# A graph kernel on one core: the row of numbers for the degree one-hots moves from SBUF into a PSUM bank

## The reference

```python
xn = _layernorm(x)
# layer 0, graph part: theta(x_dst - x_src) + phi(x_src), relu, max over the edges of a node
e = relu((xn[dst] - xn[src]) @ theta.T + theta_b + xn[src] @ phi.T + phi_b)
x = x + where(isfinite(segment_max(e, dst)), ..., 0) + mix0(xn)   # mix0: attention over features, MLP
x = x + experts(layernorm(x))                                     # 8 experts, gated
# layer 1, graph part: three rounds of a mean over neighbours; the mean needs the degree of each node
deg = segment_sum(ones, dst)
mean = segment_sum(h[src], dst) / maximum(deg, 1)
x = x + sage(...) + mix1(...); x = x + ffn(layernorm(x))
```

## Time and profile before

| | us |
|---|---|
| median of three runs | 2274.82 |
| the profiled execution, device time | 2287.81 |
| span of its trace, first to last instruction | 2286.0 |
| PE / DVE / ACT / POOL busy in the span | 1742.0 / 1300.6 / 594.1 / 1173.6 |
| mean granted TensorE clock | 0.849 |
| POOL gathers L273, x400, busy | 523.9 |
| DVE scans L526, x399, busy | 192.9 |

### The profile page before, as it was taken

The page is one execution under the profiler, slowest core; times in us unless marked ns, Lnnn a source line. Parts: engine busy times, 40 slices in busy tenths (PEclk is TensorE's granted clock), DMA queues, the critical chain, the costliest instruction groups (busy, mean ns, idle before and its releaser), DMA issues. The chain is left out here.

```text
span 2286.0 us, 25612 instructions
## 1 busy us (share of the span) xinstructions
PE 1742.0 (76%) x8399; PEld 1010.7 (44%) x8399; DVE 1300.6 (57%) x2567; ACT 594.1 (26%) x937; POOL 1173.6 (51%) x888
## 2 busy tenths in 40 slices
PE   7985454635552746999999259699989999997996
PEld 6862122212221513555555138655565556544543
DVE  6878666766775644777777244545541221115995
ACT  4001001100111124666666131321120010003453
POOL 0888888878886777888888857300000000000343
PEclk9557777777785868999999667899999999997998
DMA  6257688887868202111110020154424443531002
GB/s 171 62 141 196 184 222 216 216 228 211 227 191 206 60 2 51 36 34 33 33 33 13 1 66 2 19 124 108 108 50 119 126 96 92 127 79 38 1 7 78
DMA packets 193170, 229.06 MB, mean 100 GB/s; under 512 B 66574, under 2 KB 174178, under 8 KB 187697
## 3 DMA queue, kind: packets, MB, share of 16 engines
q1 hardware_dynamic: 125887, 172.58, 28.2%
q0 software_dynamic: 67200, 55.46, 11.0%
HBM read 148.81 MB, written 78.24 MB: 99 GB/s over the span
## 5 line engine op out<-in xcount | busy, mean ns | idle before, releaser
L706 POOL DMA_INDIRECT adjacency<-all_cell_val,all_cell_idx x400 | 546.3, 1366 | 151.2 <-issue 120.4
L273 POOL DMA_INDIRECT edge_ring<-b_rows,all_src_idx x400 | 523.9, 1310 | 174.3 <-issue 172.5
L1659 POOL TENSOR_TENSOR ffn_hl<-ffn_hid,ffn_hh 128x448 f16<-128x448 f32 x56 | 70.0, 1252 | 737.9 <-ACT ffn_hid L1676 737.9
L1472 PE MATMUL bank<-sage_adj,sage_zh 125*128 125x448 f16 x1050 | 370.1, 352 | 3.4 <-DVE sage_zl L1526 3.4
L1472 PE MATMUL bank<-sage_adj,sage_zl 125*128 125x448 f16 x1050 | 370.0, 352 | 0.0
L526 DVE SCALAR_TENSOR_TENSOR edge_ring<-edge_ring,w_keep 125x256 f32<-125x256 f32 x399 | 192.9, 484 | 142.6 <-DMA edge_ring<-b_rows,all_src_idx 122.3
L1549 DVE TENSOR_TENSOR sage_u<-bank,w_rd 128x448 f32<-128x448 f32 x42 | 26.2, 624 | 236.2 <-PE bank L1477 233.4
L1472 PEld LDWEIGHTS bank<-sage_adj,sage_zh 125*128 125x128 f16 x1050 | 102.6, 98 | 101.8 <-issue 8.0
L1472 PEld LDWEIGHTS bank<-sage_adj,sage_zl 125*128 125x128 f16 x1050 | 102.7, 98 | 99.6 <-issue 5.8
L681 DVE SCALAR_TENSOR_TENSOR edge_junk<-bank,all_key_c,all_later 125x400 f16<-125x400 f32 x232 | 145.6, 627 | 0.0
L820 PE MATMUL bank<-all_a,w_W1h 128*128 (+1 forms) x448 | 122.5, 355 | 25.0 <-ACTq L1115 25.0
(11 more groups left out here) (423 smaller groups left out, 3598.8 us busy)
## 6 DMA issues: line engine op xcount, KB each, us to landing
sage_adj<-adjacency SPq DMA_DIRECT2D x105, 490.0 KB
run_max<-edge_ring SPq DMA_DIRECT2D x40, 1120.0 KB
adjacency<-edge_zero SPq DMA_DIRECT2D x25, 714.0 KB
experts_gb<-gate_rows SPq DMA_DIRECT2D x56, 224.0 KB
edge_ring<-b_rows,all_src_idx POOLq DMA_INDIRECT x400
adjacency<-all_cell_val,all_cell_idx POOLq DMA_INDIRECT x400
sage_adj<-adjacency SPq DMA_DIRECT2D x105, 56.9 KB
run_max<-edge_ring SPq DMA_DIRECT2D x40, 130.0 KB
```

The costliest lines, as they stand in the source:

```text
L273: nc.gpsimd.indirect_dma_start(ring[:, k % RING, :], None, dram.rows[:, :], bass.IndirectOffsetOnAxis(ap=c.src_idx[:, k:k + 1], axis=0)).t ...
L706: nc.gpsimd.indirect_dma_start(dram.adj_flat, bass.IndirectOffsetOnAxis(ap=c.cell_idx[:, k:k + 1], axis=0), c.cell_val[:, k:k + 1], None). ...
L1472: ins = mm(ps[4 * b + h][:, 0:T], z[:, g * JG + j, half(h)], adj[g][:, j, :], start=(g == 0 and j == 0 and z is zh), stop=False)
L1659: nc.gpsimd.tensor_tensor(hl[:, m, :], hid[:, m, :], hh[:, m, :], ALU.subtract).then_inc(low, 1)
```

## The change

A row of 125 numbers is copied to PSUM once, into the last columns of bank 6, and both comparisons read it there. So that bank 6 holds nothing else meanwhile, the `b` rows take banks 4, 5 and 7 in turn, and `b_rows(j)` waits for copy j-3 instead of j-4.

```diff
+        b_bank = lambda j: (4, 5, 7)[j % 3]
+        row_p = ps[6][0:B, 2 * D - P:2 * D - P + B]
...
                     pe.wait_ge(taken, 4 * (j // 4) + 4)
-                    if j >= 4:
-                        pe.wait_ge(b_out, j - 3)
+                    if j >= 3:
+                        pe.wait_ge(b_out, j - 2)
                     for k in range(KH):
-                        ins = mm(ps[4 + j % 4][0:B, 0:D], c.yn[:, k, B * j:B * (j + 1)], wb[:, k, :], start=(k == 0), stop=(k == KH - 1))
+                        ins = mm(ps[b_bank(j)][0:B, 0:D], c.yn[:, k, B * j:B * (j + 1)], wb[:, k, :], start=(k == 0), stop=(k == KH - 1))
...
-                            nc.scalar.copy(xt[:, j, :], ps[4 + j % 4][0:B, 0:D]).then_inc(b_out, 1)
+                            nc.scalar.copy(xt[:, j, :], ps[b_bank(j)][0:B, 0:D]).then_inc(b_out, 1)
...
                 dve.wait_ge(edges_in, 80)
+                v.tensor_copy(row_p, c.row[0:B, 0:B])
                 v.tensor_copy(src_f[:], c.src_idx[:])
...
                         v.tensor_tensor(oh_hi[:, e, :], hi[:, e].unsqueeze(2).to_broadcast([B, 5 * HOT, NB]),
-                                        c.row[0:B, 0:NB].unsqueeze(1).to_broadcast([B, 5 * HOT, NB]), ALU.is_equal)
+                                        row_p[:, 0:NB].unsqueeze(1).to_broadcast([B, 5 * HOT, NB]), ALU.is_equal)
...
                     v.tensor_tensor(oh_lo[:, g % 2], lo[:, g * HOT:(g + 1) * HOT].unsqueeze(2).to_broadcast([B, HOT, B]),
-                                    c.row_b[:].unsqueeze(1).to_broadcast([B, HOT, B]), ALU.is_equal).then_inc(hot_ready, 1)
+                                    row_p.unsqueeze(1).to_broadcast([B, HOT, B]), ALU.is_equal).then_inc(hot_ready, 1)
```

## The result

Five runs of the change took 2257.4 to 2259.92 us, median 2259.52; before, beside them, 2276.1 us. The medians lie 16.6 us apart; the ratio, which is not that of the medians, is 0.992, 95% interval 0.9903 to 0.9937. A later set on another chip gave 0.994 (0.9925 to 0.9955). The forecast was 2261.2 us, a gain of 13.6 us and a ratio of 0.994.

A forecast was written before the change was run, and what follows sets the result against it. GpSimd issuing 400 gathers was taken to bound the stage, losing 28.0 us early to stretches. A 14.4 us gain at gather 49 less 0.8 for later stretches made 13.6: 2274.8 to 2261.2 us, range 2252 to 2274.

The forecast's parts named there:

- The place of the row: Early gathers starting inside comparisons: reading the row from PSUM ends their stretching, worth 0 to 28.0 us.
- What was late next: Gathers 44 to 49 wait for TensorE to free `xn` tiles; gather 49 starts at 142.1, a gain of 14.4 us.
- TensorE's turns and the comparison's price: In the gather stage, TensorE's turns stay 3.84 us and a comparison reading a bank costs 0 extra.
- rival 4: Comparisons read a broadcast row from a bank at half rate, 4.3 instead of 2.15 us: slower, 2301 us; chance 4%.
- The copy and the banks: Row copy takes 0.3 us, hidden by a 2.22 us wait; three banks for b rows cause no wait, at most 2.2.
- Behind gather 49: Later gathers: ring slots suffice, VectorE catches up, and denser scans add 0.8 us of stretches, bounds 0 and 3.
- The stages behind the barrier: Stages after the gather stage hang on its end and on nothing absolute; no size given.
- Rival 1: The row's place is of no account, something else in the comparison blocks GpSimd: time 2274.8 us; chance 5%.
- Rival 2: Gain is real in the gather stage but partly given back behind it: 2265 to 2269 us; chance 15%.
- Rival 3: TensorE's turns run at full clock, gather 49 starts at about 131: a gain of 25, 2250 us; chance 5%.

The follow-up runs named there:

- three kernels with more room for tiles of `xn` or earlier `grams`: Against the change: ring of 56 slots, 2254.57 us; extra grams every sixth turn, 2257.12; ring of 56 with extra grams every tenth turn, 2246.42.
- the longer ring with the old comparisons: Kernel before with a ring of 56 slots in batches of 8 instead of 50 in batches of 10, comparisons reading SBUF: 2273.09 us, ratio 0.999.

## Why the prediction was right

**The place of the row.** Forecast: 27 stretched gathers become bare, a term of at most 28.0 us. Measured: the stretches fall from 28.0 to 0.8 us. The kernel with oh_hi alone in the bank shows both behaviours side by side, and the one with the banks and the copy alone rules out every other part of the change. The first of the two statements in the Trainium skill's page "SBUF — State Buffer", section "Who interferes with whom", that a VectorE instruction with two SBUF inputs contends with a GpSimd instruction that reads SBUF, agrees with the traces: 27 of 27 gathers were held in the kernel before, 23 of 23 beside 0 of 6 with oh_hi alone in the bank. By that section's inference about building descriptors gathers would not have been held, and they were.

**What was late next.** Forecast: from gather 44 on TensorE sets the pace, and gather 49 starts at 142.1. Measured: gather 44 is the first that waits, 0.9 us beyond its issue, the five behind it wait 2.3 each, and gather 49 starts at 142.73. Of the 0.6 us, 0.4 is that `grams(24)` ended at 142.19 instead of 141.80, in an execution that began its first `b` products 0.8 us later, ahead of every changed wait; 0.2 is that gather 49 starts 0.54 us after the matmuls' end and not 0.30. The three kernels with more room for tiles of `xn` or earlier `grams` show that this wait is what held the other half: they win 5 to 12 us at gather 49 or 55 over the change, and at the last gather they have 4.5 to 11 of it.

**TensorE's turns and the comparison's price.** Forecast: 3.84 us a turn and 0 for the bank. Measured: 3.84, and a median of 2232 ns where it was 2236. The comparison is no slower with its broadcast row in a bank, which removes rival 4.

**The copy and the banks.** Forecast: 0.3 us, hidden, and no wait. Measured: the copy takes 0.28 us, and the fourth product of the first group doesn't wait. PE and ACT there:

```profile
21.64 3.62 PE L298 MATMUL bank<-early_wb,all_yn 128*125 128x256 f32 x16
```

```profile
22.70 0.37 ACT L425 COPY edge_ring<-bank 125x256 f32<-125x256 f32 x1 [0.18 <-PE bank L298]
```

Four products take 3.62 us as in the earlier trace rows, and the first copy ends at 23.07, before the fourth product is due at 21.64 + 2.61 = 24.25. With only oh_lo changed, three banks too, gather 0 started at 54.49.

**Behind gather 49.** This is the step that was off, in sign: forecast 0.8 us of additional stretches; measured 2.5 us fewer (9.5 us from gather 49 on, where the profile before had 11.9). With the 13.8 us of gather 49 that makes the 16.3 of the last gather, against 13.6 in the sum. The 11.9 that I took for the kernel's value was one draw: in ten executions the stretches from gather 49 on lay between 8.5 and 14.4 us. The four with oh_lo in SBUF had 9.8 (banks and copy only), 11.9, 12.6 and 14.4, the six with oh_lo in the bank 8.5 to 10.6. So a part of some 2 us may be the change's own; one execution each can't tell it from scatter, and its cause was not tried. The direction of the reasoning (denser scans stretch more) was not seen in any of them. That the set on the other chip gave 0.994, the forecast to the digit, is therefore partly luck: the forecast had a term of the wrong sign, and the two sets differ by more than that term.

**The stages behind the barrier.** The two profiled spans differ by 29.8 us, though the last gather is only 16.3 us earlier. The 13.5 us left over are one execution's: from the first gather of the next stage to the end the profile before took 1573.6 us; banks and copy only, with the old comparisons, 1563.5; the longer ring with the old comparisons 1559.4; the change 1560.3 and 1561.0. The other five lie between 1558.6 and 1568.6. Whoever had compared only the two spans would have found nearly twice the gain. What makes these 15 us was not tried; they are seen chiefly between the experts and the first mean over neighbours: from the end of TensorE's last matmul of the experts to its first with the adjacency it is 224.2 us in the profile before, 213.3 to 217.9 in the nine others.

**The rivals.** Rival 1 fell with the first profile. Rival 2 (part given back behind the stage) can't be seen: by their ratios two sets put the gain at 18 and 13.7 us, on either side of the 16.3 us at the last gather. Rival 3 didn't come: TensorE's clock was at half speed in the turns as before (0.54 over the stretch).

## What to carry to other kernels

When GpSimd issues indirect DMAs one after another and sets the length of a stage, look at their durations against VectorE's timeline: here those that started inside a comparison with two SBUF inputs began their own 1.21 us only at its end, and one of the two inputs in PSUM freed them at no cost to the comparison. Before counting the whole of such a stretch as gain, follow each gather's other waits: here half of the 28 us turned into a wait for tiles that TensorE hands over at its own pace, and that half came only with room in the ring and an earlier order of TensorE. A buffer that gives nothing today (ratio 0.999) can be worth 5 us (by the ratios) to 8.5 (at the last gather) once the wait ahead of it is gone, so it is worth trying again after each gain.

## What the runs showed of the hardware

- The hold is one-sided. In the kernel before a comparison takes 2.23 to 2.24 us whether gathers start inside it or not, and follows the one before without a gap while a gather is being held. The 27 held gathers end 1.08 to 1.25 us after the comparison in which they started. They do this even where the next comparison reads SBUF too and is already running: the gather at 67.87 in the earlier trace rows starts in the first of three such comparisons, ends at 69.71, and does its 1.21 us inside the second.
- The hold bears on the start of a gather only. In the kernel before ten gathers were already open, by 0.1 to 0.5 us, when such a comparison started; all ten took 1.21 to 1.22 us, and the comparisons 2.23 to 2.24. POOL and DVE there:

```profile
74.33 1.21 POOL L273 DMA_INDIRECT edge_ring<-b_rows,all_src_idx  x1 [0.31 <-issue]
```

```profile
74.45 2.24 DVE L536 TENSOR_TENSOR early_oh_lo<-early_lo,all_row_b 125x2000 bf16<-125x2000 f32 x1 [1.51 <-PE bank L311]
```

- Scans of 0.48 us, with both inputs in SBUF, stretch gathers by up to 0.26 us. With about the same scans, the sum of stretches over the last 351 gathers was 8.5 to 14.4 us from one execution to the next. That this is a matter of where the starts happen to fall is likely, but not shown.
